# Key offsets of a graph kernel in two bits a quarter, five superblocks to a register word, loaded in three parts near the beginning

## What is computed

```python
h = relu(layernorm(x))
def conv(h, W, b):
    h = h @ W
    return segment_sum(h[src] * norm, dst) + b        # norm = dinv[src] * dinv[dst], self loops added
x = x + conv(relu(conv(relu(conv(h, W1, b1)), W2, b2)), W3, b3)
h = relu(layernorm(x))
red = segment_sum(h[src] + relvectors[edge_type], dst)
x = x + gru_cell(red, h, w_ih, w_hh, b_ih, b_hh)
```

## Time and profile before

| | |
|---|---|
| median of 3 runs | 944.51 us (944.26 to 945.32) |
| the profiled execution: its time | 944.24 us |
| its span on the core | 940.3 us |
| mean granted TensorE clock | 0.979 of full speed |
| PE busy | 892.0 us (95%) |
| DVE busy | 449.7 us (48%) |
| ACT busy | 284.0 us (30%) |
| POOL busy | 24.2 us (3%) |

### The profile page before, as it was taken

How to read it: one execution, slowest core, us unless ns; L and a number is a source line. 1 busy time by engine, 2 the same in 40 slices (tenths; PEclk the granted TensorE clock), 3 DMA queues, 4 the chain that set the end, 5 groups by cost and what they waited for, 6 DMA issues and landing times.

```text
span 940.3 us, 17459 instructions
## 1 busy us (share of the span) xinstructions
PE 892.0 (95%) x6300; PEld 561.4 (60%) x6300; DVE 449.7 (48%) x1157; ACT 284.0 (30%) x558; POOL 24.2 (3%) x41
## 2 busy tenths in 40 slices
PE   2789997999999999999999999999999999999996
PEld 1358886989999875444444544444454455555553
DVE  8865886888888511011112313334344133334336
ACT  3355554556655411010111212222132121122122
POOL 0220000000000000000000000000000000000000
PEclk8779998999999999999999999999999999999999
DMA  7000000000000310000000101111401000000011
GB/s 215 3 2 1 8 14 7 18 15 13 14 14 20 117 54 1 1 1 1 1 0 23 40 12 45 46 45 46 140 19 31 2 28 28 23 23 23 23 33 31
DMA packets 27356, 27.76 MB, mean 30 GB/s; under 512 B 3217, under 2 KB 25901, under 8 KB 27272
## 3 DMA queue, kind: packets, MB, share of 16 engines
q1 hardware_dynamic: 26600, 26.18, 8.7%
q10 hardware_dynamic: 672, 0.41, 0.2%
HBM read 17.43 MB, written 9.15 MB: 28 GB/s over the span
## 4 chain that ended last, share of the span: by engine, by line
PE 92%; DVE 5%; issue 1%; ACT 1%; DMA 0%; SPq 0%; DVEq 0%
PE ps L1152 42%; PE ps L859 14%; PE ps L585 9%; PE ps L766 8%; PE ps L1163 5%; PE ps L589 5%; PE ps L1183 2%; PE ps L840 2%; DVE node_b L868 1%; PE ps L770 1%; PE ps L808 1%; PE ps L783 1%; PE ps L828 1%; PE ps L570 1%; PE ps L781 0%
## 5 line engine op out<-in xcount | busy, mean ns | idle before, releaser
L1152 PE MATMUL ps<-count,node_b 128*128 128x512 f16 (+3 forms) x1400 | 271.2, 351 | 0.4 <-DVE node_b L1314 0.3
L766 PE MATMUL ps<-node_b 128*128 128x175 f16 x808 | 195.7, 256 | 21.1 <-issue 16.8
L859 PE MATMUL ps<-node_a,count 128*128 128x256 f16 (+1 forms) x1050 | 213.4, 274 | 0.2 <-DVE node_a L982 0.2
L1152 PEld LDWEIGHTS ps<-count,node_b 128*128 128x128 f16 (+2 forms) x1400 | 121.4, 97 | 142.4 <-issue 8.2
L868 DVE TENSOR_TENSOR node_b<-node_b 128x1024 f16<-128x1024 f16 (+2 forms) x303 | 161.6, 589 | 0.0
L1065 ACT ACTIVATE count<-ps 128x500 f32 x202 | 122.8, 608 | 118.4 <-PE ps L766 115.0
L1152 PE MATMUL ps<-count,node_a 128*128 128x512 f16 (+3 forms) x700 | 135.4, 352 | 0.0
L770 PE MATMUL ps<-params 128*128 128x20 f16 x808 | 134.2, 179 | 0.0
L1152 PEld LDWEIGHTS ps<-count,node_a 128*128 128x128 f16 (+1 forms) x700 | 60.0, 97 | 74.1 <-issue 6.8
L859 PEld LDWEIGHTS ps<-node_a,count 128*128 128x128 f16 (+1 forms) x1050 | 96.5, 101 | 5.5 <-issue 0.7
L766 PEld LDWEIGHTS ps<-node_b 128*128 128x128 f16 x808 | 80.0, 99 | 32.4 <-issue 20.8
(11 more groups left out here) (209 smaller groups left out, 803.3 us busy)
## 6 DMA issues: line engine op xcount, KB each, us to landing
node_a<-in_x SPq DMA_DIRECT2D x4, 768.0 KB, 7.3
table_scratch<-agg SPq DMA_DIRECT2D x21, 128.0 KB, 1.7
node_b<-table_scratch SPq DMA_DIRECT2D x3, 768.0 KB, 7.5
xt<-x_scratch SPq DMA_DIRECT2D x16, 128.0 KB, 2.1
out<-scaled SPq DMA_DIRECT2D x16, 128.0 KB, 1.7
xt<-in_x SPq DMA_DIRECT2D x12, 128.0 KB, 2.1
params<-in_x SPq DMA_DIRECT2D x12, 128.0 KB, 2.1
x_scratch<-xt SPq DMA_DIRECT2D x12, 128.0 KB, 1.7
```

Of the source, the lines that this page charges most:

```text
L766: return PE.matmul(window(s)[:, :, first], low, key_hot[k][:, j, :, i].rearrange("p (t w) -> p t w", w=SPAN), start=(s == 0 and j == 0), s ...
L859: last = PE.matmul(out_slot(u)[0:m, :], count[0:k, t, u * P:u * P + m], node_a[0:k, t, part, :], start=(t == 0 and part == 0), stop=(t == ...
L1152: last = PE.matmul(ps[:, b, 0:cols], nodes[0:k, t, part, f * P:(f + 1) * P], count[0:k, t, c * CHUNK:c * CHUNK + cols], start=(n == 0 and ...
```

## The change

The offsets of a superblock now take 6 bits in place of 10. The origin of a quarter lies 2 to 5 nodes behind that of the quarter before (`most` and `least` cut it to that, one quarter after the other), so two bits hold each step; five superblocks go into a word, 41 words in place of 68. PE loads 11 of them ahead of the verdict, 18 behind the branch, and 12 at superblock 4. DVE's key rows are made in another order: `key_and_node` writes 7 times the source's tile plus the destination as f32, in two instructions of 128x512, while the origins are worked out, and one subtraction of 128x1024 makes the f16 keys at the end. The verdict's rule on steps is now only on the gap behind the last quarter. `row_min` is worked out behind the packing of the words, not ahead of it.

```diff
-PACK, PACK_BITS = 3, 10
-OFFSET_LOADS = (22, 22, 24)
+PACK, PACK_BITS = 5, 6
+STEP_LEAST, STEP_MOST = 2, 5
+OFFSET_LOADS, LAST_WORDS_AT = (11, 18, 12), 4
...
-            for pad, value in ((src_row[:, Q - 1, :], -1), (rel_row[:, Q - 1, :], -1), (next_row[:, :], N), (dst_row[:, Q - 1, :], N - 1),
-                               (asked, 1.0), (not_asked, 0.0)):
+            for pad, value in ((src_row[:, Q - 1, :], -(1 << 17)), (rel_row[:, Q - 1, :], -1), (next_row[:, :], N), (asked, 1.0), (not_asked, 0.0)):
                 DVE.memset(pad, value).then_inc(pads_set, 1)
+            for j in range(QUARTERS):
+                DVE.memset(dst_row[:, Q - 1, j * P:(j + 1) * P], N - (QUARTERS - j) * STEP_LEAST).then_inc(pads_set, 1)
...
             DVE.tensor_scalar(neg_first, dst_row[:, :, 0], -1.0, None, ALU.mult).then_inc(firsts_negated, 1)
...
+            def most(j):
+                DVE.wait_ge(*dve_seq.now)
+                DVE.scalar_tensor_tensor(out=origin[:, :, j], in0=origin[:, :, j - 1], scalar=float(STEP_MOST),
+                                         in1=dst_row[:, :, j * P] if j < QUARTERS - 1 else last_origin,
+                                         op0=ALU.add, op1=ALU.min).then_inc(*dve_seq.up())
+            def least(j):
+                DVE.wait_ge(*dve_seq.now)
+                DVE.scalar_tensor_tensor(out=origin[:, :, j], in0=origin[:, :, j - 1], scalar=float(STEP_LEAST), in1=origin[:, :, j],
+                                         op0=ALU.add, op1=ALU.max).then_inc(*dve_seq.up())
+            def key_and_node(q):
+                DVE.scalar_tensor_tensor(out=key_f[:, q, :], in0=high_row[:, q, :], scalar=float(SPAN), in1=dst_row[:, q, :],
+                                         op0=ALU.mult, op1=ALU.add).then_inc(*dve_seq.up())
...
+            least(1)
+            key_and_node(0)
+            most(2)
+            key_and_node(1)
+            least(2)
+            DVE.tensor_copy(first_node, dst_row[:, :, 0]).then_inc(*dve_seq.up())
+            most(3)
...
+            least(3)
+            DVE.wait_ge(*dve_seq.now)
+            DVE.tensor_tensor(origin_steps, origin[:, :, 1:QUARTERS], origin[:, :, 0:QUARTERS - 1], ALU.subtract).then_inc(*dve_seq.up())
...
+            DVE.tensor_tensor(key_r.rearrange("p q (j e) -> p (q j) e", e=P), by_quarter,
+                              origins.unsqueeze(2).to_broadcast([P, Q * QUARTERS, P]), ALU.subtract).then_inc(keys_made, 1)
...
             DVE.tensor_reduce(row_max, parts, AX_X, ALU.max).then_inc(*dve_seq.up())
+            DVE.wait_ge(words_turned, 1)
...
+            DVE.tensor_tensor(offsets, offsets, offsets_high, ALU.bitwise_or).then_inc(offsets_made, 1)
             DVE.tensor_reduce(row_min, parts, AX_X, ALU.min).then_inc(*dve_seq.up())
...
             last.then_inc(words_turned, 1)
+            PE.wait_ge(offsets_made, 1)
+            offset_words.extend(load_offsets(0))
             PE.wait_ge(verdict_summed, 1)
             PE.matmul(ps[0:1, 5, 0:1], verdict[:, :], ones[:, 0:1], start=True, stop=True).then_inc(judged, 1)
...
-            PE.wait_ge(offsets_made, 1)
-            offset_words = [*load_offsets(0), *load_offsets(1)]
+            offset_words.extend(load_offsets(1))
...
-                if s == OFFSET_LOADS[0] * PACK:
-                    offset_words += load_offsets(2)
+                if s == LAST_WORDS_AT:
+                    offset_words.extend(load_offsets(2))
```

More of the change, by code:

```diff
@@ L140, in program @@
         tile_ends = early(SETTLES)
-        rules = early(RULES * Q * QUARTERS + 3 + SETTLES)
+        rules = early(3 * Q * QUARTERS + Q + 3 + SETTLES)
         assert at[0] <= T * CW
@@ L406, in prepare_dve @@
-            DVE.tensor_scalar(offsets_high, words[:, :, 2], float(1 << 2 * PACK_BITS), None, ALU.mult).then_inc(*dve_seq.up())
+            DVE.wait_ge(words_turned, 1)
+            DVE.tensor_scalar(words, ps[0:1, 6, 0:OFFSETS * PACK].rearrange("p (w i) -> p w i", i=PACK), -float(STEP_LEAST * (1 + 4 + 16)), None,
+                              ALU.add).then_inc(*dve_seq.up())
+            DVE.wait_ge(*dve_seq.now)
+            size = float(1 << PACK_BITS)
+            for i in (0, 2):
+                DVE.scalar_tensor_tensor(out=words[:, :, i], in0=words[:, :, i + 1], scalar=size, in1=words[:, :, i],
+                                         op0=ALU.mult, op1=ALU.add).then_inc(*dve_seq.up())
@@ new lines, in prepare_dve @@
+            DVE.tensor_scalar(offsets_high, words[:, :, 4], size ** 4, None, ALU.mult).then_inc(*dve_seq.up())
+            DVE.wait_ge(*dve_seq.now)
+            DVE.scalar_tensor_tensor(out=offsets, in0=words[:, :, 2], scalar=size ** 2, in1=words[:, :, 0],
+                                     op0=ALU.mult, op1=ALU.add).then_inc(*dve_seq.up())
+            DVE.wait_ge(*dve_seq.now)
+            DVE.tensor_tensor(offsets, offsets, offsets_high, ALU.bitwise_or).then_inc(offsets_made, 1)
+            DVE.tensor_reduce(row_min, parts, AX_X, ALU.min).then_inc(*dve_seq.up())
@@ L425, in prepare_dve, with load_offsets @@
             DVE.tensor_copy(verdict_i[:, :], ps[0:1, 5, 0:1]).then_inc(verdict_in, 1)
+        offset_words = []
+        def load_offsets(nth):
+            first, n = sum(OFFSET_LOADS[:nth]), OFFSET_LOADS[nth]
+            return nc.values_load_multi_w_load_instructions(
+                offsets[:, first:first + n], engines=[mybir.EngineType.PE], min_val=0, max_val=(1 << PACK * PACK_BITS) - 1,
+                skip_runtime_bounds_check_because="each step was cut to its two bits")[1]
+        def span_of(s, j):
+            if j == 0:
+                return slice(0, SPAN)
+            word, at_bit = offset_words[s // PACK], s % PACK * PACK_BITS
+            steps = (word >> at_bit) & 3
+            for before in range(1, j):
+                steps = steps + ((word >> (at_bit + 2 * before)) & 3)
+            return bass.ds(nc.s_assert_within(steps + STEP_LEAST * j, 0, WINDOW - SPAN,
+                                              skip_runtime_bounds_check_because="origins are at most WINDOW - SPAN behind the first node"), SPAN)
         def prepare_pe():
@@ L724, in load_starts @@
                 skip_runtime_bounds_check_because="the verdict above: every start is a destination, 0 to N - 1")[1]
-        def load_offsets(nth):
-            first, n = sum(OFFSET_LOADS[:nth]), OFFSET_LOADS[nth]
-            return nc.values_load_multi_w_load_instructions(
-                offsets[:, first:first + n], engines=[mybir.EngineType.PE], min_val=0, max_val=(1 << PACK * PACK_BITS) - 1,
-                skip_runtime_bounds_check_because="the verdict above: offsets are 0 to WINDOW - SPAN, in their bits")[1]
-        def offset(words, s, j):
-            if j == 0:
-                return slice(0, SPAN)
-            word, at_bit = words[s // PACK], s % PACK * PACK_BITS
-            if j == 1:
-                return bass.ds((word >> at_bit) & 7, SPAN)
-            third = (word >> (at_bit + 3)) & 15
-            return bass.ds(nc.s_assert_within(third if j == 2 else third + ((word >> (at_bit + 7)) & 7), 0, WINDOW - SPAN,
-                                              skip_runtime_bounds_check_because="origins are at most WINDOW - SPAN behind the first node"), SPAN)
         def lanes(q):
```

72 lines of the change are left out of this document (29 added, 43 removed).

## The result

The changed kernel takes **935.12 us** (median of 4 runs, 934.27 to 935.86), the kernel before 944.64 beside it (4 runs, 944.26 to 945.32): ratio 0.9898, 95% interval 0.9881 to 0.9915.

What follows compares the result with a forecast made beforehand. PE was taken to set the time from 164.3 to 320 us. The profiled 944.24 less 1.5 (up to superblock 66) and 7.6 (superblock 66) gave 935.1, with 0.27 for the median 935.4 us; range 930.5 to 939.0.

Steps and rivals of the forecast that it cites:

- Bound and superblock 66: PE sets the time from 164.3 to 320 us; moving the last load away from superblock 66 gives -7.6 us.
- The price of a register: PE's register loads: 0.2365 us a register, no fixed part; loads of 11, 18 and 12 cost 2.60, 4.26 and 2.84.
- +2.7: Ahead of superblock 4: PE's queue runs dry during the load of 12, 2.84 us, little of it absorbed.
- B: Rival: the clock falls for a short while in the new gap at superblock 4, +2.4 us, 937.8; chance 0.20.
- C: Rival: the clock falls there and stays down until the first weights' matmuls, +13.0 us, 948.4; chance 0.05.
- DVE up to the verdict: DVE's reordered work ahead of the verdict: its sum at 19.34 us against 17.80, +1.5 for all five engines.
- The load ahead of the verdict: PE's load of 11 ends 0.45 us behind the sum and delays the verdict's matmul: +0.5 us.
- PE's start: The load of 18 behind the branch: superblock 0 begins at 25.4 us in place of 29.64, 4.2 earlier.
- The margin of 0.3 us at superblock 2: DVE's second one-hots end at 28.1 us, PE comes at 30.4; up to a microsecond can be lost.
- Rival D: The clock fares better from 58.9 us on, giving back 4 us: 931.4; chance 0.14.
- The 27 register instructions more: New shifts and masks on PE's sequencer in 202 superblocks: no visible cost, PE being gapless from 164 us on.
- The early part: Everything up to superblock 66 together: -1.5 us, bounds -3.5 and +1.

Runs made afterwards that it cites:

- e5_last_off_by_4: The changed kernel with loads of 12, 18 and 11 registers in place of 11, 18 and 12, so the last begins 4 bytes later: 939.56 us.
- e11: The changed kernel unaltered, run again in a later set: 936.04 us.
- e7: The kernel before, its old words put on a multiple of 16 bytes by one word of padding, loads of 24, 20 and 24: 932.45 us.
- e8: The kernel before with its old words and also ACT's table `starts` on a multiple of 16 bytes: 932.16 us.
- e12: e7 unaltered, run again in the same set as e11: 932.92 us.

## Why the prediction was right, point by point

The time was right by luck: one term was mis-sized by 2 us, and others made up for it.

- **Bound and superblock 66: right.** From 65 to 68 the lead grows by 7.68 us (forecast 7.6), and PE is gapless there at full clock.
- **The price of a register: the step that failed.** "the time is proportional, with no fixed part to see" was read from three loads that all began off a multiple of 16 bytes. For 11 and 18 registers it held (2.83 and 4.29 against 2.60 and 4.26), for the 12 at superblock 4 it was 2.0 us too high. The term "+2.7" for superblock 4 measured +0.84 (from superblock 3 to 4 the lead goes from 2.66 to 1.82). Rivals B and C had no gap to fall into; e5_last_off_by_4 supplies the gap of 2.41 us, and B happens: 1.8 us for the gap and 1.5 behind it, where B had 2.4.
- **DVE up to the verdict: mis-sized.** Forecast +1.5 and +0.5, measured +3.3. Of it 0.7 is outside the change: the source indices landed at 6.40 in place of 5.70. In e11, the same kernel, DVE began on them at 5.70 and the cast came at 20.79, 2.7 behind the kernel before. Some 0.5 is DVE and PE: four turned words took 1.01 us, not 0.74, and the unpacking 1.34, not 1.15. The load ahead of the verdict ended 0.62 behind the sum (forecast 0.45).
- **PE's start: right in kind**, 26.55 and not 25.4, for the 1.3 us by which the cast missed its forecast. The margin of 0.3 us at superblock 2 was indeed used up: a wait of 0.20 for the one-hots.
- **Rival D came in part.** Over 57.4 to 70.7 us the clock is 0.72 where it was 0.50, and superblock 12 comes 0.85 us sooner for it.
- **The 27 register instructions more, said to "cost nothing I can see": not borne out, cause open.** From superblock 107 to 200 the new words lose 0.83 to 0.95 us against the kernel before in all ten traces that have them, in single steps of up to 0.18 us; with old words it is 0.26, 0.0 and 0.24 (e7, e8, e12). So it goes with the new words. The row of fused register instructions (FUSED_REGOPS at the line of `sources`, 606 in both) reads 52/53/53 ns after against 37/46/59 before, which may be it, but no run took that apart.
- **The sum** was right since the errors cancel, which is luck: forecast -1.5 and -7.6, that is -9.1; measured -2.8, -7.7, +0.9 and +0.5 at the end, -9.0 (from the unrounded numbers). The early part's -2.8 is itself made of errors: the last load gave 1.9 us and rival D 0.85 more than forecast, PE's start 1.1 and small steps 0.3 less.

## What to carry to other kernels

Before cutting the number of registers, look at where their words begin: a load from a multiple of 16 bytes cost under a third, and a word of padding gave more than a new encoding that needed a longer way to make. A price fitted to three rows holds for what the three have in common. And a start moved ahead of what its supplier can feed is worth nothing, or less, where the idle time behind it brings the clock down.

## What the runs showed of the hardware that was not expected

A register load's time goes by its first word's address. Off a multiple of 16 bytes (4, 8 and 12 alike): 6, 11, 18, 22, 24 and 29 registers in 1.49, 2.64, 4.29, 5.20, 5.68 and 6.88 us, 0.24 to 0.25 each. On it: 4 (ACT), 12, 20, 24 and 28 in 0.31, 0.85, 1.36, 1.63 and 1.90 us, 0.26 to 0.27 for each four more; 13 took as long as 16, 1.12 us. The load ahead of the verdict took 0.2 us more than these in every kernel that has one (2.83 for 11, 1.04 for 12). The 6 at 8 above a multiple have four words within that begin on one, and paid in full. ACT's loads follow the same rule (0.91 and 0.31 us for four). The Trainium skill, Runtime: NRT & Kernel Launch ("Instruction fetch mechanics"), has some 200 ns a register for loads from HBM; these are from SBUF, and come near it only off the multiple. The Trainium skill, SBUF — State Buffer ("Operand start alignment"), says of its rule that it is about legality and that its runs timed nothing; here the start is legal everywhere and decides a factor of 3.5.

The clock of a trace can't be trusted ahead of its first record. e7 and e12 are one kernel; over 18 to 28 us the one reads 1.00, with its first record at 27.2 us, and the other 0.50 to 0.53, with one at 14.2, and the eight matmuls of 128x404 in that stretch take 2.82 and 2.89 us, where the next eight take 1.56 in both. The lengths of like rows tell the speed there.
